# Heads paired on TensorE in two packed attentions, with unread products ahead of their first batch

## The reference, cut to what matters

```python
attn = jnp.einsum('bhqd,bhdk->bhqk', q * scale, k)
attn = jnp.where(kv_mask[:, :, None, :], attn, -jnp.inf)
attn = jax.nn.softmax(attn, axis=-1)
mean = jnp.einsum('bhqk,bhkd->bhqd', attn, v)
ex2 = jnp.einsum('bhqk,bhkd->bhqd', attn, v * v)
std = jnp.sqrt(jax.nn.relu(ex2 - mean * mean))
```

```python
q = layer_norm(q, ln_q_g, ln_q_b)
kv = layer_norm(kv, ln_kv_g, ln_kv_b)
attn = jnp.einsum('bhqd,bhkd->bhqk', Q, K) / math.sqrt(DH)
ctx = jnp.einsum('bhqk,bhkd->bhqd', jax.nn.softmax(attn, axis=-1), V)
r = jnp.transpose(ctx, (0, 2, 1, 3)).reshape(B, Tq, C) @ Wo + q
```

## Time and profile before

| what | value |
|---|---|
| median of 3 runs | 2608.34 us (2588.43 to 2613.47) |
| the profiled execution, time | 2597.26 us |
| its span, first to last instruction | 2595.5 us |
| mean granted TensorE clock | 0.932 of full |
| PE busy | 2261.8 us, 87% of the span |
| DVE busy | 1783.5 us, 69% |
| ACT busy | 1481.9 us, 57% |
| POOL busy | 718.5 us, 28% |

### The profile page before, as it was taken

One profiled execution on the slowest core, in us unless ns is written; L12 is line 12 of the kernel. 1 busy time (PEld: TensorE's weight loads), 2 busy tenths in 40 slices (PEclk: granted clock), 3 DMA queues, 4 the chain that ended last, 5 costly groups with the idle time before them and its releaser, 6 DMA issues. The chain is left out here.

```text
span 2595.5 us, 53248 instructions
## 1 busy us (share of the span) xinstructions
PE 2261.8 (87%) x17289; PEld 1802.1 (69%) x17289; DVE 1783.5 (69%) x4693; ACT 1481.9 (57%) x4021; POOL 718.5 (28%) x1041
## 2 busy tenths in 40 slices
PE   4999999995999999979788885899998787888896
PEld 3898989984989899969655553566665784555553
DVE  5666666667666666666577775888886654777746
ACT  2554545553555555557366765677777553666656
POOL 2111111111111111020245442666665104333200
PEclk7999999997999999989799997999999895999978
DMA  4100011000000100010000001000000000000000
GB/s 118 22 21 22 21 22 54 22 21 21 8 23 13 22 21 21 1 33 0 7 10 8 10 5 66 7 0 5 16 15 10 4 5 7 9 8 8 3 3 32
DMA packets 72941, 47.12 MB, mean 18 GB/s; under 512 B 29232, under 2 KB 71601, under 8 KB 72753
## 3 DMA queue, kind: packets, MB, share of 16 engines
q1 hardware_dynamic: 72752, 44.62, 6.5%
HBM read 41.45 MB, written 2.10 MB: 17 GB/s over the span
## 5 line engine op out<-in xcount | busy, mean ns | idle before, releaser
L1725 DVE TENSOR_REDUCE maxima<-bank 128x2 f32<-128x512 f32 x512 | 343.6, 684 | 176.3 <-PE bank L934 174.3
L1405 ACT ACTIVATE probs_t<-bank 128x512 f32<-128x512 f32 x512 | 292.0, 600 | 73.0 <-PE bank L925 68.3
L1281 ACT ACTIVATE wide_probs_t<-bank 128x256 f32<-128x256 f32 x256 | 98.5, 385 | 310.5 <-PE bank L814 308.3
L2047 POOL TENSOR_TENSOR wide_columns<-wide_pair_columns,zero 128x8 f32<-128x8 f32 x16 | 4.4, 278 | 861.4 <-DVE x L1622 816.5
L925 PE MATMUL bank<-q_packed,k_packed 32*128 32x256 f32 x1024 | 209.3, 351 | 31.3 <-ACT probs_t L1405 31.1
L1286 ACT ACTIVATE wide_probs<-bank,wide_neg_max 128x129 f32<-128x129 f32 x512 | 184.1, 365 | 84.7 <-DVE wide_neg_max L1592 80.4
L934 PE MATMUL bank<-k_packed,q_packed 32*128 32x256 f32 x1024 | 209.5, 352 | 8.3 <-DVE k_packed L1738 5.0
L1293 ACT ACTIVATE wide_heads_high<-bank,wide_columns 128x128 fp32r<-128x128 f32 x512 | 160.3, 365 | 96.6 <-PE bank L826 95.3
L925 PEld LDWEIGHTS bank<-q_packed,k_packed 32*128 32x128 f32 x1024 | 127.2, 200 | 120.7 <-ACT probs_t L1405 62.5
L1597 DVE RECIPROCAL wide_inverse<-wide_sums 128x2 f32<-128x2 f32 x256 | 42.5, 166 | 224.6 <-ACT wide_probs L1286 224.6
L1611 DVE SCALAR_TENSOR_TENSOR wide_heads_low<-bank,wide_columns,wide_heads_high 128x128 fp32r<-128x128 f32 x512 | 155.1, 344 | 40.9 <-ACT wide_heads_high L1293 35.5
(11 more groups left out here) (296 smaller groups left out, 6900.5 us busy)
## 6 DMA issues: line engine op xcount, KB each, us to landing
cn<-in_ctx SPq DMA_DIRECT2D x48, 128.0 KB, 2.0
wide_pair_weights<-in_L_xattn_wq SPq DMA_DIRECT2D x16, 256.0 KB, 2.9
wide_pair_weights<-in_L_xattn_wk SPq DMA_DIRECT2D x16, 256.0 KB, 3.3
wide_pair_weights<-in_L_xattn_wv SPq DMA_DIRECT2D x16, 256.0 KB, 3.8
wide_pair_weights<-in_L_xattn_wo SPq DMA_DIRECT2D x16, 256.0 KB, 3.6
q_packed<-max_rows SPq DMA_DIRECT2D x256, 4.0 KB
wide_ctx_rows<-in_ctx SPq DMA_DIRECT2D x4, 512.0 KB, 5.3
x<-in_x SPq DMA_DIRECT2D x4, 512.0 KB, 6.3
```

The source lines that it names most:

```text
L1405: act.activation(probs_t[j % 8][:, :], shifted_bank[j % 2][:, :], ACT.Exp, bias=0.0).then_inc(s.exp_ready, 1)
L1725: dve.tensor_reduce(maxima[pack // 2][:, b, pack % 2, :], head_scores[packed_scores(1 - u, j)][:, :].rearrange("p (a k) -> p a k", a=UNITS ...
```

## The change

In both packed stages PE's side steps move behind odd heads only, so that the products of heads 2k and 2k+1 follow each other with nothing between. The steps of ACT and DVE get numbers of their own. In the second packed stage the preparation of rows starts one batch earlier (`fifth` for `fourth`, `fourth` for `coming`). In the first, the result is turned behind head 15 and copied by ACT in the next window, POOL's order changes, and `sums_copy` has a fifth place. In windows where there is neither a batch nor one behind it (five per stage) PE makes one product of 128x512 per step that nobody reads.

```diff
-SCHEDULE1 = Schedule(place_k=0, project_k=2, turn=(6, 7), values=9, place_q_first=11, place_k_first=14, result=12)
-SCHEDULE3 = Schedule(place_k=1, project_k=3, turn=(6, 7), values=9, place_q_first=11, place_k_first=10, result=15)
...
+SCHEDULE1 = Schedule(second_q=(1, 2), second_k=(1, 3), project_q=(5, 6, 7), project_k=(5, 7, 8), turn=((9, 10), (9, 11)),
+                     values=(11, 12), first_q=(13, 14), first_k=(13, 14), result=(15, 0))
+SCHEDULE3 = Schedule(second_q=(1, 2), second_k=(1, 3), project_q=(3, 4, 5), project_k=(5, 6, 7), turn=((7, 8), (9, 11)),
+                     values=(9, 10), first_q=(11, 12), first_k=(11, 12), result=(15, 0))
+SQUARES = (10, 12)
+PLACED_ROWS, TURNED_BACK, HEADS = (13, 15), (13, 14), (13, 14)
...
+                    if not core and not carry:
+                        pe.matmul(shifted_bank[j % 2][:, :], place[:, 0, 0, :], place[:, 0, :, :].rearrange("p g d -> p (g d)"),
+                                  start=True, stop=True)
...
-                    if third and coming and (j == PLACE_Q if following else j == PROJECT_Q):
-                        pe.wait_ge(s.turned_copied, i + 4)
-                    if following and j == PLACE_Q:
-                        if ahead or third:
-                            pe.wait_ge(s.q_ready, 2 * (n + 1) + 1)
-                        put("q", 1, upper)
...
+                    if following and j == when.second_q[0]:
+                        pe.wait_ge(s.q_ready, 2 * (n + 1) + 1)
+                        if third and fourth:
+                            pe.wait_ge(s.turned_copied, i + 5)
+                        put("q", 1, upper)
...
                     for unit in range(UNITS):
-                        if carry and j == when.turn[unit]:
+                        if carry and j == when.turn[unit][0]:
...
-                    if following and j == when.values:
+                    if following and j == when.values[0]:
...
-                    if ahead and j == when.place_q_first:
+                    if ahead and j == when.first_q[0]:
                         pe.wait_ge(s.q_low, n + 3)
                         if following:
                             pe.wait_ge(s.v_taken, n + 2)
                         put("q", 0, upper)
-                    if carry and not third and j == when.result:
+                    if ahead and j == when.first_k[0]:
+                        pe.wait_ge(s.k_low, n + 3)
+                        if carry:
+                            pe.wait_ge(s.heads_taken, heads_taken(third, n))
+                        put("k", 0, lower)
+                    if third and fifth and j == PLACED_ROWS[0]:
+                        pe.wait_ge(s.placed, 2 * (i + 6))
+                        if ahead:
+                            pe.wait_ge(s.q_ready, 2 * (n + 2) + 1)
+                        else:
+                            after(pe, s.turned_copied, i + 5)
...
+                    if carry and not third and j == when.result[0]:
                         pe.wait_ge(s.heads_ready, UNITS * n)
+                        if ahead:
+                            pe.wait_ge(s.k_ready, 2 * (n + 2) + 1)
                         for m in range(2):
                             for unit in range(UNITS):
                                 last = pe.transpose(lower[:, (2 * m + unit) * P:(2 * m + unit + 1) * P],
                                                     heads_out[unit][:, m * P:(m + 1) * P], ident[:, :])
                         last.then_inc(s.result, 1)
...
+                    if third and coming and j == TURNED_BACK[0]:
+                        pe.wait_ge(s.rows_normed, i + 4)
+                        if ahead:
+                            pe.wait_ge(s.k_ready, 2 * (n + 2) + 1)
...
+                        for m in range(4):
+                            last = pe.transpose(lower[:, m * P:(m + 1) * P], norm_packed[:, m // 2, m % 2 * P:(m % 2 + 1) * P], ident[:, :])
+                        last.then_inc(s.turned_back, 1)
...
+                    if late and not third and j == when.result[1]:
+                        act.wait_ge(s.result, n - 1)
...
+                    if third and fifth and j == PLACED_ROWS[1]:
+                        act.wait_ge(s.turned, i + 6)
+                        after(act, s.rows_normed, i + 5)
+                        act.activation(turned_packed[:, :, :].rearrange("p k c -> p (k c)"), upper[:, :], ACT.Copy).then_inc(s.turned_copied, 1)
...
-                    if third and fourth and j == 15:
-                        act.wait_ge(s.turned, i + 5)
-                        after(act, s.rows_normed, i + 4)
...
-                if coming and j == 12:
+                if coming and j == 3:
...
+                if fourth and j in (3, 4):
+                    for k in (2 * (j - 3), 2 * (j - 3) + 1):
+                        dve.wait_ge(s.turned_copied, i + 5)
+                        if j == 3:
...
-                if coming and j == 5:
-                    dve.wait_ge(s.measured, 4 * (i + 4))
...
-                coming, fourth = (at(o) is not None for o in (3, 4))
+                fourth, fifth = (at(o) is not None for o in (4, 5))
+                if fifth:
...
+                    pool.tensor_tensor(placed_packed[:, 0, :], x[:, ds(at(5), 1), :].rearrange("p a d -> p (a d)"),
+                                       positions[:, :], ALU.add).then_inc(s.placed, 1)
...
-                if coming:
-                    chain = Chain(pool, s.rstd_ready, RSTD_STEPS * (i + 3))
+                    chain = Chain(pool, s.rstd_ready, RSTD_STEPS * (i + 4))
...
-                    pool.wait_ge(s.aggregated, 4 * (i + 4))
+                    pool.wait_ge(s.aggregated, 4 * (i + 5))
...
-                    after(pool, s.turned_back, i + 3)
+                    after(pool, s.turned_back, i + 4)
```

More of the change, by code:

```diff
@@ L191, in __init__ @@
         self.moments_chain = sem(f"{name}_moments_chain")
+        self.mask_copied = sem(f"{name}_mask_copied")
         self.vn_chain = sem(f"{name}_vn_chain")
@@ L899, in window @@
                 i = n - B * third
-                core, following, carry, ahead, coming, fourth = (at(o) is not None for o in (0, 1, -1, 2, 3, 4))
-                late = at(-2) is not None
+                core, following, carry, ahead, coming, fifth = (at(o) is not None for o in (0, 1, -1, 2, 3, 5))
+                fourth, late = (at(o) is not None for o in (4, -2))
                 def turn_maxima(m, half):
@@ L1352, in window @@
                 i = n - B * third
-                core, following, carry, ahead, coming, fourth = (at(o) is not None for o in (0, 1, -1, 2, 3, 4))
+                core, following, carry, ahead, coming, fifth, late = (at(o) is not None for o in (0, 1, -1, 2, 3, 5, -2))
                 for j in range(HN):
@@ L1987, in own @@
                 for unit in range(UNITS):
-                    if carry and j == SCHEDULE3.turn[unit] + 1:
+                    if carry and j == SCHEDULE3.turn[unit][1]:
                         sums = side[unit][:, :].rearrange("p (h e) -> p h e", h=HN)
@@ L2137, in window @@
                         scratch = heads_t[unit][:, 0:P]
-                        moments.link(pool.tensor_tensor(scratch, mean, mean, ALU.mult))
+                        Chain(pool, s.moments_chain, UNITS * (n - 1) + unit).link(pool.tensor_tensor(scratch, mean, mean, ALU.mult))
                         pool.tensor_tensor(square, square, scratch, ALU.subtract).then_inc(s.heads_ready, 1)
+                if coming:
+                    if following:
+                        pool.wait_ge(s.v_projected, n + 2)
+                    pool.sem_inc(idle, 1)
+                    pool.tensor_scalar(keys_in[1 - u], scratch_keys, key_mean[:, 0:1], None, ALU.add).then_inc(s.in_ready, 1)
                 if following:
```

212 lines of the change are left out of this document (94 added, 118 removed).

## The result

The changed kernel is slower by 1.2%. Its median is 2620.23 us (2605.19 to 2635.02, 20 runs), that of the kernel before 2586.74 us (2577.89 to 2613.47, 20 runs beside them); the ratio is 1.0119, 95% interval 1.0099 to 1.0139, so 26 to 36 us more. The prediction said 2571 us, with 2545 to 2604 as its range for 8 in 10, and gave 0.07 to slower.

What follows compares the result with a forecast made beforehand. PE, busy 87% of the span, was taken as nearest to the bound. First stage -16.6 us and second -12 gave -28.6 on the profiled 2597.26, or 2568.7, given as 2571 us; range for 8 in 10: 2545 to 2604.

Steps and rivals of the forecast that it cites:

- Pairs, first stage: First packed stage: pairing heads saves PE 1.36 us a batch; with other savings and waits, 19.34 becomes about 17.85 us.
- The wait for the values behind head 13: First packed stage: the `put` of q waits for DVE's `v_taken`, leaving PE idle 1.3 us a batch.
- Entry of the first stage: Unread products delay it 8 us; first two batches give back 6.7; third batch entered 2 us late.
- The bound of 0.24 us for an unread product: Time of one 128x512 product at the full clock, from two 256-column products 0.12 us apart; 0.48 at half clock.
- The second stage: Second packed stage: batches go from 21.27 to 20.5 us, and a slow late batch gives 3 us, -12 in all.
- ACT's copy held for 1.6 us: Second packed stage: ACT's copy to `turned_packed` waits about 1.6 us a batch for POOL's normalization.
- PE idle for 2.0: Second packed stage: PE waits about 2 us a batch at head 1 for head 15's exponential, behind ACT's held copy.
- the clock falls in each batch: Rival, 0.20: new holes lower the clock, 1.2 us a batch in the first stage, 0.8 in the second; 2597 us.
- Entry of the second stage: Products added about 4 us, earlier preparation spared time, the held copy gave it back: 0, range -8 to +4.
- POOL's chain sets the pace there: Entry of the second packed stage: POOL's chain was taken to set the pace before and after the change.
- slower: Rival, 0.08: whole second-stage batches at a low clock, +5.5 us each, 2623 to 2634 us; outcome above 2634 given 0.07.
- a clock under 0.95 in the steady batches: Sign that the forecast is wrong and that the rival of a clock falling in each batch holds.

Runs made afterwards that it cites:

- e1: The changed kernel without its unread products, the rest of the change kept; 2596.16 us, ratio 1.0037 to the kernel before.
- f4: First packed stage in the changed order without unread products, second stage written as in the kernel before; 2571.52 us, ratio 0.9927 to the kernel before.
- e4: The changed kernel with two `turned_packed` tiles in turn, normalized in place, no `norm_packed`, so no hold; 2554.15 us, ratio 0.9881 to the kernel before.
- f1: Two tiles in turn as above, unread products kept, but ACT's copy of the rows in 32 pieces of 16 columns; 2619.49 us, ratio 1.0097 to the kernel before.
- e5: The changed kernel run once more, unaltered, for a second profile; 2616.34 us.
- e7: Two tiles in turn, unread products kept, but ACT's copy of the rows in 8 pieces of 64 columns; 2551.41 us, ratio 0.9848 to the kernel before.

## Why the prediction was wrong, point by point

- **Pairs, first stage: right, a little small.** Forecast 17.85 us a batch; at the full clock 18.1 to 18.4, and 18.8 on average, since the clock fell in about every other batch. (The forecast's own terms, 1.36 and 0.1 saved and 0.1 more of waits, give 17.98; 17.85 took 0.13 too much, 1.6 us over twelve batches.) The wait for the values behind head 13 was forecast at 1.3 us and was 1.4. The stage as a whole gave 15 to 18 us; forecast 18.6, the entry left out.
- **Entry of the first stage: the delay right, what it gives back wrong.** Forecast 8 us late, seen 7 to 10. But the first batch was to take 18.5 us at the full clock, and took 23.60 at 0.58, against 22.28 at 0.57 before: the fall came later, not less. Only the second batch kept its forecast (17.9; 17.92 at 0.99). The bound of 0.24 us for an unread product (0.48 at the half clock) holds for products in a row (0.23 and 0.43 from start to start); between two heads it costs 0.72 at the half clock and takes the pair's overlap as well. That step had been costed as columns alone.
- **The second stage: every wait right, their price wrong.** ACT's copy held for 1.6 us: it was 1.7. PE idle for 2.0: it was 2.0, at the head forecast. Batches at the full clock 20.5: they were 20.8 to 21.1. What failed is the term for the clock. I counted the hole at its length, and had a rival in which the clock falls in each batch, at 0.8 us a batch more; the fall costs 2.9 to 3.0 us (1.5 in the batches at 0.92). A batch of 20.5 forecast and 23.9 measured is what made the stage lose. In e1 all ten batches fell (238.0 us, 0.86), in f4 some did (219.0, 0.93): 19 of the 28 us by which the two lie apart, and 6 more stand in entry 2 (60.4 and 54.7). The price was not new either: the kernel before had a hole of 2.0 us too, kept 0.96 in one profile and 0.92 in the other, and there its batches took 20.9 us at 1.00, 22.0 at 0.92 and 23.6 at 0.86. The change made the dear kind the rule. Why the old batches mostly bore the hole and the paired ones don't was not tested. The paired ones have less PE work beside the hole (16.7 of 20.8 us against 18.2 of 21.3), which is an argument and no more.
- **Entry of the second stage: wrong.** Forecast 0 (-8 to +4), seen +17 to +21. In the first profile: 3.3 us to the first turning (2120.77, after `vn` at 2117.4), which the prediction had as 4; 3.4 for one more preparation ahead of the first scores (32.4 us from first turning to first scores, 29.0 before); 8.6 in the window of the first scores (30.8 us against 22.2); and 2.0 at the first exponential, behind the held copy. The parted pairs are only part of the 8.6: with the same unread products and no hold e4 took 21.5 us there, at a clock of 0.78 where it was 0.56; f1, with the hold alone put back, 28.7 at 0.59; e1, held and without unread products, 23.9 at 0.64. How hold, products and clock share it is not shown. The step that failed is that POOL's chain sets the pace there: it does up to the first scores, and from there on PE's own products do, parted and mostly at the half clock. The held copy cost more, too, than the 8 us that it was counted at (0 with it, -8 without): between e4 and f1 the hold alone made the entry 12.5 us longer (55.9 and 68.4).
- **The number of unread products.** I counted 80 a stage. The condition also holds in the last window, so 16 more stand behind the last batch (192 in the trace). They cost little, if anything: the rest of the program behind the second stage took 70.0 to 73.1 us in the profiles with them and 68.2 to 71.4 in those without.
- **The base.** The sum was made on an execution of 2597 us; twenty runs give 2587. On that base the same sum is 2558, so the error hid some of the miss: 49 us by the two times, 60 by the difference (-29 forecast, +31 seen).
- **The rivals.** The time fell near that of "slower", 2623, but not by its mechanism, whole batches at the half clock. It was "the clock falls in each batch" with a price of 3 in place of 0.8 in the second stage, together with the two entries. Each of these was in the text; their sum, not one of them, set the time. The prediction's own sign of that rival, a clock under 0.95 in the steady batches, is there (0.90).
- **What stays open.** In the profiles the entries and the two stages together grew by 5 to 28 us, by which of the two of each kernel one takes (733.6 and 744.7 before, 750.0 and 761.8 after), and the medians differ by 33. At least part of it is that both profiles of before had a second stage 7 to 13 us longer than the same code in f4, most of it in the two late batches.

## What to carry to other kernels

A wait of 2 us in a batch of 20 costs its length only while TensorE's clock stays up; test what it costs by adding such a hold alone, and look for tiles that can be used in turn before reordering the work. When a step is moved a batch earlier, its buffers have to follow: the same two tiles, used in turn and normalized in place, turned a loss of 1.2% into a gain of 1.2%. Products that are added to keep TensorE busy lie on the path as soon as something behind them is ready, and must not stand between products that would otherwise start together.

## What the runs showed of the hardware that I had not expected

- The cost of a hold is far from proportional: 0.4 us on ACT cost 0.33 us a batch at a clock of 1.00, 1.9 us cost 4.5 at 0.87.
- A product over the whole array between two products in groups of 32 rows: at the half clock head and product take 1.44 us with 512 columns and 1.13 with 128, where two heads in a row take 0.73 together.
- ACT's small copies are cheap one behind the other: 0.60 us for 512 columns at once, 1.02 in 8 pieces, 2.53 in 32, so 0.06 us for each piece more.
- The same entry of the first stage, with the same instructions, took 35.6 us at a clock of 1.00 in e5 and in e7, and 43.2 at 0.78 in e4 and f1. In e7 the clock fell behind the window of the first scores, in e4 and f1 within it (0.62 there); whether the kernel or the single execution settles it is not shown, as only the changed kernel has two profiles (35.5 and 35.6).
